# Moving copies, weight loads, one projection and two row sums in an eight-core recurrent layer

## The reference

```python
xn = layernorm(x)
shifted = pad(xn)[:, :L];  delta = shifted - xn
x5 = tanh((xn + delta * x0_mu) @ x0_w.T)            # five groups of 32
mix = einsum(x5, x2_w) + x_bias                     # r, w, k, v, g
r = (xn + delta*mix_r) @ r_w.T                      # k, v, g likewise
w = -exp(tanh((xn + delta*mix_w) @ w_w1.T) @ w_w2.T + w_b2)
o = chunked_recurrence(r, k, v, w, bonus)           # 4 heads, chunks of 32 tokens
s = (groupnorm(o) * silu(g)) @ o_w.T
h = silu(xn @ w_gate.T) * (xn @ w_up.T)             # 3072 wide, int32 weights / 127
out = x + s * silu(h @ w_down.T)
```

## Time and profile before

| what | value |
|---|---|
| three runs | 1733.5, 1734.38, 1734.84 us, median 1734.38 |
| the profiled execution's own time | 1731.29 us |
| its span (slowest core, core 1) | 1729.7 us |
| spans of cores 0 to 7 | 1720.8, 1729.7, 1724.3, 1728.6, 1723.0, 1709.1, 1713.0, 1725.8 us |
| TensorE busy | 1674.3 us, 97% |
| VectorE, ScalarE, GpSimd busy | 63%, 28%, 11% |
| HBM | 348.56 MB read, 44.04 MB written |

### The profile page before, as it was taken

The page is one execution under the profiler, slowest core; times in us unless marked ns, Lnnn a source line. Parts: engine busy times, 40 slices in busy tenths (PEclk is TensorE's granted clock), DMA queues, the critical chain, the costliest instruction groups (busy, mean ns, idle before and its releaser), DMA issues.

```text
span 1729.7 us, 26524 instructions; the slowest of 8 cores (1709.1 to 1729.7 us)
## 1 busy us (share of the span) xinstructions
PE 1674.3 (97%) x9248; PEld 779.7 (45%) x9248; DVE 1087.2 (63%) x1844; ACT 480.7 (28%) x806; POOL 195.3 (11%) x408
## 2 busy tenths in 40 slices
PE   5999799999999999999999999999999999999998
PEld 2444344445444454344544445444454445544454
DVE  5565655656757476564875647757476485764856
ACT  1143211333114321143211432114321143212421
POOL 3112301112011020110200001000110001100000
PEclk9999899999999999999999999999999999999999
DMA  8999899997699777998436974465734355354422
GB/s 164 177 169 177 203 237 160 155 196 210 140 172 181 212 220 176 192 195 266 171 105 168 219 270 153 126 191 151 264 122 165 128 179 211 117 183 146 177 65 107
DMA packets 79234, 303.47 MB, mean 175 GB/s; under 512 B 10687, under 2 KB 15232, under 8 KB 73728
## 3 DMA queue, kind: packets, MB, share of 16 engines
q0 software_dynamic: 27456, 95.08, 34.2%
q10 hardware_dynamic: 25344, 124.79, 20.5%
q1 hardware_dynamic: 26304, 81.90, 13.7%
HBM read 348.56 MB, written 44.04 MB: 227 GB/s over the span
## 4 chain that ended last, share of the span: by engine, by line
PE 82%; DMA 11%; DVE 3%; issue 1%; DVEq 1%; POOL 1%; SPq 0%; ACT 0%; POOLq 0%; ACTq 0%
PE PB L1240 17%; PE PB L1245 16%; PE PB L1365 8%; PE PB L1354 7%; PE PB L1505 7%; PE PB L1528 6%; PE PB L1397 6%; DMA sb_gu<-w_gu 3%; PE PB L1450 3%; PE PB L1466 3%; DMA sb_wd<-kept_wd 3%; DMA sb_gu<-kept_gu 2%; DMA sb_wd<-w_fd 1%; DMA kept_gu<-sb_gu 1%; PE PB L1273 1%
## 5 line engine op out<-in xcount | busy, mean ns | idle before, releaser
L1240 PE MATMUL PB<-sb_xnT,sb_gu 128*128 128x512 bf16 x1536 | 366.2, 381 | 14.6 <-DMA sb_gu<-w_gu 5.9
L1245 PE MATMUL PB<-sb_xnT,sb_gu 128*128 128x512 bf16 x1536 | 364.3, 380 | 0.0
L920 DVE SCALAR_TENSOR_TENSOR sb_xin<-PB,sb_xb,sb_dT 128x512 bf16<-128x512 f32 x320 | 218.1, 744 | 172.8 <-PE PB L1273 172.7
L691 ACT ACTIVATE sb_scr<-PB 128x512 bf16<-128x512 f32 x192 | 113.8, 597 | 529.8 <-PE PB L1245 510.0
L1245 PEld LDWEIGHTS PB<-sb_xnT,sb_gu 128*128 128x128 bf16 x1536 | 150.8, 98 | 182.7 <-issue 3.3
L1240 PEld LDWEIGHTS PB<-sb_xnT,sb_gu 128*128 128x128 bf16 x1536 | 140.7, 98 | 201.8 <-issue 57.2
L852 DVE SCALAR_TENSOR_TENSOR sb_hall<-PB,sb_scr 128x512 bf16<-128x512 f32 x192 | 130.8, 685 | 125.7 <-ACT sb_scr L691 125.7
L1365 PE MATMUL PB<-sb_wd,sb_hall 128*128 128x512 bf16 x768 | 178.6, 381 | 10.0 <-DMA sb_wd<-w_fd 5.2
L1354 PE MATMUL PB<-sb_wd,sb_hall 128*128 128x512 bf16 x768 | 179.4, 383 | 6.6 <-DMA sb_wd<-w_fd 6.0
L459 POOL DMA_DIRECT2D sb_gu<-w_gu x106 | 57.5, 543 | 619.0 <-PE PB L1245 539.9
L700 ACT ACTIVATE sb_wc<-PB 128x512 bf16<-128x512 f32 x64 | 38.2, 597 | 316.2 <-PE PB L1365 316.2
(11 more groups left out here) (155 smaller groups left out, 1683.7 us busy)
## 6 DMA issues: line engine op xcount, KB each, us to landing
sb_gu<-w_gu POOLq DMA_DIRECT2D x106, 512.0 KB, 10.4
sb_gu<-kept_gu ACTq DMA_DIRECT2D x86, 512.0 KB, 5.3
sb_wd<-kept_wd ACTq DMA_DIRECT2D x56, 768.0 KB, 7.4
sb_ring<-kept_ring ACTq DMA_DIRECT2D x34, 1024.0 KB, 6.7
sb_xin<-x SPq DMA_DIRECT2D x48, 512.0 KB, 8.3
kept_gu<-sb_gu SPq DMA_DIRECT2D x24, 512.0 KB, 9.0
sb_ring<-w_g POOLq DMA_DIRECT2D x20, 512.0 KB, 13.8
sb_ring<-w_v POOLq DMA_DIRECT2D x16, 512.0 KB, 14.0
```

The lines of the kernel that those rows point to most:

```text
L691: e.activation(out=sb_scr[:, p, :], in_=GB[p][:], func=AF.Silu, bias=0.0, scale=INV127).then_inc(a_silu, 1)
L920: e.scalar_tensor_tensor(out=sb_xin[:, p, c, :], in0=PM[j][:], scalar=sb_xb[:, n, c:c + 1], in1=sb_dT[:, c, :], op0=ALU.add, op1=ALU.mult) ...
L1240: e.matmul(GB[p][:], sb_gu[:, sl, 0, c, :], sb_xnT[:, c, :], start=(c == 0), stop=(c == NC - 1))
L1245: i = e.matmul(UB[p][:], sb_gu[:, sl, 1, c, :], sb_xnT[:, c, :], start=(c == 0), stop=(c == NC - 1))
```

## The change

Four parts. On SP, the copies of units 4 and 5 stand ahead of the small replicating copies. On ACT, groups 0 to 2 of the first down half are issued after the SiLUs of units 14, 15 and 16, and group 3 after the first half of v. On PE, in step t = 2 of the first tile alone, the transpose and the output projection of token block 0 stand ahead of both down units. At the start, ACT makes the row sums of blocks 1 and 3 and DVE those of 0 and 2, and POOL makes the variance from the sums for blocks 1 and 3.

```diff
@@ sync_program
         for it in range(N_MT):
             nxt = it + 1 < N_MT
+            keep_gu(it, 4)
+            keep_gu(it, 5)
             replicate_x5(it, IR)
             replicate_x5(it, IK)
             replicate_x5(it, IV)
-            for hc in range(4, 9):
+            for hc in range(6, 9):
                 keep_gu(it, hc)
@@ pool_program, ln_rstd
-            if it == 0:
-                e.wait_ge(v_lbn, n + 1)
+            if it == 0 and j % 2 == 0:
+                e.wait_ge(v_lbn, j // 2 + 1)
...
-            e.wait_ge(a_stat, n - 3)
-            e.wait_ge(v_xnt, n - 3)
+            stats = n - 1 if it else j // 2 + 1
+            e.wait_ge(a_stat, stats)
+            if it:
+                e.wait_ge(v_xnt, n - 3)
@@ scalar_program
         def ln_stat(it, j):
             n = 4 * it + j
-            src = x_ln[j % 2]
-            e.wait_ge(d_x[j % 2], 16 * (n // 2))
-            e.wait_ge(p_ln, n - 3)
-            e.wait_ge(v_h, NHC * it)
+            if it:
+                src = x_ln[j % 2]
+                e.wait_ge(d_x[j % 2], 16 * (n // 2))
+                e.wait_ge(p_ln, n - 3)
+                e.wait_ge(v_h, NHC * it)
+            else:
+                src = x_first[j]
+                e.wait_ge(d_x[1] if j == 1 else d_xp[1], 16)
...
+        ln_stat(0, 1)
         for j in range(NST):
+            if j == 1:
+                ln_stat(0, 3)
             e.wait_ge(t_xn, j + 1)
...
             for hc in range(14, 17):
                 silu_gu(it, hc)
+                load_wd(it, 0, hc - 14)
...
-                load_wd(it, 0, 2 * half)
-                load_wd(it, 0, 2 * half + 1)
                 if half == 0:
+                    load_wd(it, 0, 3)
                     silu_gu(it, 17)
                     silu_gu(it, 18)
@@ vector_program
         first_stat(0)
-        first_stat(1)
         ln_xnt(0, 0)
         first_stat(2)
-        ln_xnt(0, 1)
-        first_stat(3)
-        ln_xnt(0, 2)
-        ln_xnt(0, 3)
+        for j in range(1, NST):
+            ln_xnt(0, j)
@@ tensor_program
                 if t < 3:
                     scores(it, t + 1)
+                if it == 0 and t == 2:
+                    og_transpose(0, 0)
+                    ks_transpose(0, 3)
+                    out_proj(0, 0)
+                    down_first(0, 4)
+                    down_second(0, 4)
+                    down_first(0, 5)
+                    down_second(0, 5)
+                    continue
                 down_first(it, 2 * t)
```

More of the change, by code:

```diff
@@ L526, in ln_rstd @@
                             ).then_inc(p_mean, 1)
-            e.wait_ge(p_mean, n - 3)
+            e.wait_ge(p_mean, stats)
             e.tensor_tensor(out=lr[:, 2:3], in0=lr[:, 0:1], in1=lr[:, 0:1],
                             op=ALU.mult).then_inc(p_msq, 1)
-            e.wait_ge(p_msq, n - 3)
+            e.wait_ge(p_msq, stats)
             e.tensor_tensor(out=lr[:, 3:4], in0=lr[:, 1:2], in1=lr[:, 2:3],
```

## The result

The changed kernel takes 1723.28 us (median of 4 runs, 1720.86 to 1726.13), the kernel before 1733.94 in the same comparison (4 runs, 1733.5 to 1734.84): ratio 0.9937, 95% interval 0.9921 to 0.9952. That is 10.7 us less, where 7.2 were forecast; 1723.3 lies inside the range of 1720.5 to 1732.5. The profiled execution took 1720.86 us. In 31 of 176 executions one die or both ran at a mean granted clock of 0.81 to 0.98 and took 2 to 17% longer, and no ratio, interval or median here counts them.

What follows compares the result with a forecast made beforehand. PE works nearly all the span, so its DMA waits were to be won. Core 1: -3.9 - 2.7 - 6.8 + 4.5 = -8.9; core 3: -6.1; slowest span -7.2, so 1734.4 becomes 1727.2 us, range 1720.5 to 1732.5.

Steps and rivals of the forecast that it cites:

- Part 1, -3.9: Tile 0, step t = 2: the projection fills waiting time and leaves the path behind unit 4, -3.9 us.
- The rival that this gain is lost in tile 1: Casts at tile 1's units 8 and 9 land no earlier, so 3.9 us is lost: 1731.1 us, chance 0.12.
- "better clock" bound: Tile 0, 201 to 211 us: if the new order kept the full clock, 1.4 us more would go, to -5.4.
- Part 2, -2.7 to -3.4: Tile 3: waits for casts at units 8, 9 and 12 all go, -2.7 us on core 1, -3.4 on core 3.
- Part 3, gain: Waits for kept weights, mainly unit 23 of tiles 3 to 5, go: -6.8 us on core 1, -3.3 on core 3.
- a delay d of 3.3 us: Early down loads delay unit 18's cast by one and a half loads, costing +4.5 us over tiles 1 to 4.
- the first rival: The early down loads cost nothing at unit 18 (d = 0): -12.8 us, 1721.6 us, chance 0.25.
- The slower rival: Down loads hold up unit 18 in four tiles; at d = 6.7 it is +5.4, 1739.8 us, chance 0.04.
- would be wrong: Signs against the forecast, among them waits for casts at units 19 to 22 or for kept weights elsewhere.
- Part 4, hidden: Start: first gate-up unit +0.3 us, bounds -1 to +1.5, hidden under unit 4's wait, 0 to the path.
- The sum: Core 1 -8.9 us to 1720.8, core 3 -6.1 to 1722.5; slowest span falls 7.2, median to 1727.2.
- core 3 becomes the slowest: After the change core 3's span, 1728.6 to 1722.5 us, exceeds core 1's 1720.8 and sets the time.

Runs made afterwards that it cites:

- Part 1 alone: Kernel before with only the projection of token block 0 moved ahead of both down units in tile 0, step t = 2: 0.9987, second time 0.9979.
- second profile of before: The kernel before, unedited, timed and profiled again beside the last experiments: ratio to itself 1.0002.
- part 2 alone: Kernel before with only the copies of units 4 and 5 put ahead of the small replicating copies: 0.9986.
- the last experiment: Kernel before with the new projection place and copy order, and the down loads early only from tile 4 on: 0.9926, median 1720.3 us.
- part 3 alone: Kernel before with only the down loads in units 14 to 16 and group 3 after the first half of v: 1.0012.
- Parts 1 and 2 together: Kernel before with the projection moved and the copies of units 4 and 5 first, nothing else: 0.9955.
- part 3 beside the others: Changed kernel with the down loads back where they were: 0.9947 to the kernel before, against 0.9933 for the whole beside it.
- the second of the changed kernel: The changed kernel, unedited, run and profiled again beside the variants with one part left out: 0.9933 to the kernel before.

## Why the prediction was right, and where it was not

**Part 1, -3.9: right.** On core 1 step t = 2 ends with unit 5's last matmul at 225.6; before it ended, projection and unit 5 both behind unit 4, at 229.25: -3.6. Part 1 alone measured 0.9979, 3.6 us, on one chip, and 0.9987, 2.3, on another. The rival that this gain is lost in tile 1 is refuted: with part 1 alone no core waits for a cast at units 8 and 9 there. In the means over the cores tile 1 starts 3.3 us earlier (239.3, and 242.6 in the second profile of before), tile 2 2.2 earlier, tile 4 0.9, and the ends are equal; that is one execution against one, and the timings of ten executions keep 3.6 us. (The 216 us given ahead of the change for the first tile are too few: tile 1's first unit starts at 242.) The "better clock" bound gave nothing. The granted clock from 201 to 211 us is 0.83 where it was 0.53, but unit 4's last six matmuls took 1.97 us instead of 2.72 and unit 5's first twelve 3.97 instead of 2.75: the slow stretch only moved.

**Part 2, -2.7 to -3.4: right.** SP's copy goes first, and no core waits for a cast at units 8, 9 or 12 of tile 3 (the 0.4 left is DVE's). In the second profile of before these are 2.1 us, mean over the cores. The mean hides where they stand: on one core of each pair (0 and 1, 2 and 3, 4 and 5, 6 and 7), in both profiles of before the one with the longer span. They are 2.7 to 3.4 us on cores 1, 3, 4 and 7 in the first, 2.2 to 5.5 on cores 0, 3, 5 and 6 in the second, and at most 0.1 on the others. So the cores that set the time gain more than the mean does. The timing of part 2 alone, 0.9986, fits the term and does not show it by itself.

**Part 3, gain: right; cost: the step that was mis-sized.** The waits at unit 23 of tiles 3, 4 and 5 are gone on all cores. For the cost I took a delay d of 3.3 us from bounds of 0 and 6.7, "since they are issued one a unit and the third comes when the cast is all but landed". It is not so. In tile 2 all three loads are issued (533.2, 537.1, 541.0) before or while the cast of unit 18 is under way (533.53 to 549.1), and the third comes with 8 us of it still to go. There d is 15.6 - 10.1 = 5.5; in tile 3 it is 15.9 - 9.5 = 6.4, and in tile 4 3.5. Unit 18 waited 3.98, 4.73 and 0.71 us on core 1, where 1.7, 3.6 and 0.6 were forecast, so 9.4 - 1.43 = +8.0 instead of +4.5. The mean over the cores is 3.0 in tile 2 and 2.1 in tile 3. The free loads of the first rival are refuted. The slower rival needed d = 6.2 in every tile: tile 3 reached it and tile 2 came near, but in tile 1 unit 18 still did not wait and in tile 4 it lost only 0.7. There is a second item I had put under "would be wrong": the casts behind unit 18 are late as well, on four cores at unit 22 of tile 3 (2.0 to 2.2 us, and 1.0 on a fifth) and on three at unit 23 of tile 2 (2.0 to 2.2). The Trainium skill has each DMA engine go round its queues packet by packet ("DMA: Bandwidth & Descriptors", Queues, rings and completion order). The trace agrees in so far as the cast moved on during the loads (from 533 to 542 us POOL's queue took 74% of the engines' time and ACT's 18%), but 5.5 and 6.4 of the 6.7 us that the loads need by themselves were added to it. Sharing by packets was no protection here, where every load that shared was issued before the cast landed. By the waits of the table, part 3 costs 3.0 us in tile 2, about nothing in tile 3 (3.3 against the 2.6 to 3.0 of unit 23) and wins 1.6 to 2.1 in tiles 4 and 5, which the last experiment shows.

**Part 4, hidden: half right.** The forecast was +0.3 at the first unit, bounds -1 to +1.5; it was +0.7 on core 1 and +1.1 in the mean of both profiles. PE now waits 2.67, 1.32 and 2.15 us between the transposes. It was to disappear in unit 4's wait. On core 1 it did not: unit 4 starts at 46.09, after a wait of 2.34 us, and not at 45.58. But that wait varies (1.3 in the mean in before, 1.1 in the changed kernel, 2.9 in part 3 alone, which has no edit there), and the times with and without part 4 do not differ (0.9933 and 0.9939).

**The sum: the right sign, 3.5 us short.** -7.2 was forecast and -10.7 measured, although part 3's waits cost 3.5 more. That the total lies in the forecast's neighbourhood is in part luck: a cost was taken too small, and about 7 us of gain stood in no term. The timings place some of it. Parts 1 and 2 together give 0.9955, 7.8 us, where the terms had 6.6 on core 1 and 7.3 on core 3; part 3 beside the others gives 2.4 us (0.9947 to 0.9933, not clear of noise), where its waits say a loss of 1 to 2. Two things could be behind what is left, and neither is shown to be.

First, what a wait does to the clock. I had used the lower clock only as a bound of part 1, and counted a wait at its length everywhere. In the second profile of before the stretches at the lower granted clock cost 9.6 us a core (their length times a half, mean over the cores, start and last microseconds left out), and 6.2 in the changed kernel. With 52.8 us of idle time against 45.8 (stops over 0.1 us), that is -7.0 - 3.4 = -10.4, beside an end that is 8.7 earlier. But the figure goes from profile to profile: the first profile of before has 6.8, with 48.9 us idle and 5.7 in the stretches at 0.81 told of below, and the second of the changed kernel 6.6. So the clock's share lies somewhere from 0.2 to 3.4 us.

Second, "core 3 becomes the slowest" compared spans that were not alike (see below), and core 3's +4.5 was worked out with core 1's slacks, though core 3 had no wait at unit 18 of tile 3 to start from. What stays open is the share of parts 1 and 2: alone they gave 0.9987 and 0.9986 on one chip, together 0.9955 on another.

## What to carry over

Price a DMA wait by two rows, its length and the matmuls behind it; here the second added 1.6 us to a wait of 2.8. It is not paid every time. Of 138 waits of more than 2.5 us at the start of a gate-up unit (from unit 6 of tile 1 on, all cores of the fourteen profiles), 115 were followed by eight slowed matmuls and 23 were not, such as the 3.46 us above with 1.89 behind it. When loads move to another place, list every transfer that will be under way beside them, and start from the loads' own transfer time as the delay of each, unless it lands before they are issued; here it was 3.5 to 6.4 of 6.7 us. And decide per tile: the same loads at the same place cost 3 us in tile 2, where casts still run, and win 2 in tile 4, where they hardly do.

## What the runs showed of the hardware

The kernel before's first profile has a third level of the granted clock beside 1.2 and 2.4 GHz. Two windows of core 1, both with PE busy throughout (columns: stretch, length, PE, PEld, DVE, ACT and POOL busy, granted clock, DMA share, GB/s):

```profile
122.00:136.00 14.00, 14.00 (x55) 5.76 (x53) 10.57 (x17) 5.98 (x10) 0.00 (x0) 0.81 1.02 171
137.00:151.00 14.00, 13.97 (x70) 5.83 (x69) 10.23 (x13) 2.39 (x4) 6.33 (x12) 1.00 1.03 189
```

55 matmuls against 70. Cores 0 to 3 have four such stretches each, near 121, 345 and 983 us and a fourth at 556 on cores 0 and 1 and at 774 on cores 2 and 3. Every one is 15.1 us long, so 15.1 x 0.19 = 2.8 us each and 11.4 a core. Cores 4 to 7 have none, nor has any core in the other thirteen profiles. PE had been at the upper clock and busy ahead of them (from 100 to 120 us 20.00 of 20 us, at 1.00). They explain the clocks of 0.987 to 0.990 on cores 0 to 3 against 0.995 to 0.997 on the others, and 11.4 of the 23.7 us by which core 3 fell; another 5.1 are its stretches at the lower clock, 10.2 us before and 5.1 after. The Trainium skill describes a peak-current limit of 13/16, 0.81 ("TensorE: Matmul & The Clock Gate", Part 1), which takes a whole die once three of its cores run dense matmuls and holds while the load lasts. The trace agrees with the value, and with the die in that cores 4 to 7 have none; the stretch at 556 or 774 took only two of its cores. It does not show the limit holding: with eight cores busy for 97%, it was there for 60 of 1730 us on each of four cores, in one profile of fourteen. All fourteen are of executions with a mean clock of 0.98 or more on every core, so how long it lasts in others stays open.

Since it lifts the spans of cores 1 and 3, the forecast rested on a core order that was not the kernel's own. The experiments say the same: in the executions of the kernel before that were run beside them, each of the eight cores is the slowest at least once. A look at the clock of each core, and at more than one execution, should come ahead of any choice of "the slowest".
